# TensorE's order in the token stage of a fused vision-tower kernel: the score in two halves, two turns of z between them, the turned means behind the third turn

## What is computed

```python
# tokenizer: one query per patch, 16 keys and values per patch, 8 heads
reduce_feats = x.mean((3, 5))...                      # mean of each patch
q  = _ln(reduce_feats, ln_q_w, ln_q_b) @ Wq.T
kv = _ln(unf, ln_kv_w, ln_kv_b) @ Wkv.T               # every pixel
attn = softmax(einsum('bhpd,bhpnd->bhpn', q * scale, k))
aggre = einsum('bhpn,bhpnd->bhpd', attn, v)
h = reduce_feats + aggre @ proj_w.T + proj_b
# layer 0
h = h + rnn(_layernorm(h))      # tanh recurrence over the batch of 32
h = h + moe(_layernorm(h))      # 8 experts, 2 per token
```

## Time and profile before

| | before |
|---|---|
| median of 3 runs | 1656.12 us |
| profiled execution, its own time | 1680.15 us |
| its span (first to last instruction) | 1678.3 us |
| token stage, 59 full slots | 95 to 1160 us of the span |
| TensorE busy over the span | 1414.3 us, 84% |
| VectorE, ScalarE, GpSimd busy | 65%, 48%, 42% |
| granted TensorE clock, mean | 0.955 |

### The profile page before, as it was taken

How to read it: one execution, slowest core, us unless ns; L and a number is a source line. 1 busy time by engine, 2 the same in 40 slices (tenths; PEclk the granted TensorE clock), 3 DMA queues, 4 the chain that set the end, 5 groups by cost and what they waited for, 6 DMA issues and landing times. The chain is left out here.

```text
span 1678.3 us, 65455 instructions
## 1 busy us (share of the span) xinstructions
PE 1414.3 (84%) x25781; PEld 1083.8 (65%) x25781; DVE 1099.1 (65%) x3070; ACT 806.3 (48%) x2022; POOL 708.2 (42%) x858
## 2 busy tenths in 40 slices
PE   3799999999998989989898989989648888888870
PEld 2577777777777766777676667677536566555550
DVE  3567666766665767866676667777447556776773
ACT  1365565655554655555555556556443333333330
POOL 1233343333333433356655534334147734332536
PEclk9899999999998999999999999999869999999995
DMA  8977787877776876889999786673257646675866
GB/s 285 345 263 279 249 298 259 301 258 272 283 274 241 306 254 237 296 275 316 317 312 324 268 290 257 218 252 133 76 164 229 220 152 182 201 211 172 251 207 178
DMA packets 202089, 415.69 MB, mean 248 GB/s; under 512 B 25952, under 2 KB 126624, under 8 KB 201664
## 3 DMA queue, kind: packets, MB, share of 16 engines
q1 hardware_dynamic: 187504, 372.69, 64.7%
q0 software_dynamic: 14288, 38.82, 7.8%
HBM read 329.52 MB, written 81.89 MB: 245 GB/s over the span
## 5 line engine op out<-in xcount | busy, mean ns | idle before, releaser
L1039 DVE BATCH_NORM_STATS2 st<-xp 128x6 f32<-128x512 f32 x512 | 339.1, 694 | 0.5
L537 POOL TENSOR_TENSOR rs_px<-px_ve,half_neg 128x16 f32<-128x16 f32 x64 | 186.3, 2911 | 296.8 <-DVE px_ve L1044 296.8
L649 ACT ACTIVATE zT<-bank 128x512 f32<-128x512 f32 x256 | 146.2, 598 | 193.0 <-PE bank L872 192.9
L1332 POOL DMA_INDIRECT y<-ys_dram,slot x130 | 125.3, 964 | 188.4 <-DMA ys_dram<-y_s 84.4
L872 PE MATMUL bank<-ident,z_s 128*128 128x128 f32 x1024 | 163.4, 295 | 28.3 <-issue 27.5
L642 ACT ACTIVATE z_s<-bank 128x512 f32<-128x512 f32 x256 | 138.7, 597 | 61.4 <-PE bank L862 61.4
L623 ACT ACTIVATE u<-bank 128x512 f32<-128x512 f32 x256 | 132.2, 603 | 53.6 <-PE bank L812 53.6
L872 PEld LDWEIGHTS bank<-ident,z_s 128*128 128x128 f32 x1024 | 120.8, 149 | 46.9 <-issue 40.2
L832 PE MATMUL bank<-xc,u 128*32 128x64 f32 x8192 | 133.9, 220 | 18.2 <-issue 17.5
L832 PEld LDWEIGHTS bank<-xc,u 128*32 128x32 f32 x8192 | 128.0, 110 | 32.8 <-issue 21.0
L310 POOL DMA_INDIRECT xs_dram<-xrow,slot x130 | 128.4, 988 | 40.3 <-issue 37.5
(11 more groups left out here) (179 smaller groups left out, 3134.6 us busy)
## 6 DMA issues: line engine op xcount, KB each, us to landing
xp<-xpix SPq DMA_DIRECT2D x256, 512.0 KB
xc<-xg SPq DMA_DIRECT2D x256, 512.0 KB
xt<-xs_dram SPq DMA_DIRECT2D x151, 128.0 KB, 3.3
ys_dram<-y_s SPq DMA_DIRECT2D x151, 128.0 KB, 2.6
xs_dram<-zero SPq DMA_DIRECT2D x49, 384.0 KB, 8.2
base_dram<-h SPq DMA_DIRECT2D x65, 128.0 KB, 7.9
rows_dram<-tok SPq DMA_DIRECT2D x65, 128.0 KB, 7.6
hb<-base_dram SPq DMA_DIRECT2D x65, 128.0 KB, 3.0
```

The costliest lines, as they stand in the source:

```text
L537: pool.tensor_tensor(rs_px[:, :], px_ve[:, :], half_neg[:, :], ALU.pow).then_inc(s["px_done"], 1)
L649: act.activation(zT[:, c, :, :].rearrange("p h (a r t) -> p r h a t", r=2, t=TS)[:, r, :, :, :], BIG[f][:, :].rearrange("p (a h t) -> p h ...
L1039: dve.bn_stats(st[:, j, :], xp[u.x][:, 2 * j:2 * j + 2, :].rearrange("p i c -> p c i")).then_inc(s["st_done"], 1)
```

## The change

Both edits change only an order; no instruction is added or taken away, and no wait.

On TensorE `score` is cut in two calls of 64 matmuls. The waits for its inputs stand in the first, the signal `s_ps` in the second. The order was: means, score, z 0, z 1, rn, z 2, fold, z 3, xn. It becomes: means, score half 0, z 0, z 1, score half 1, z 2, rn, z 3, fold, xn. On ScalarE the copy of z 1 moves ahead of the copy of the turned means.

```diff
@@ ScalarE, slot
                 if back:
                     zT_out(act, w, 0)
+                if back:
+                    zT_out(act, w, 1)
                 if front:
                     rn_out(act, u)
                 if back:
-                    zT_out(act, w, 1)
                     zT_out(act, w, 2)
                     zT_out(act, w, 3)
@@ TensorE
-            def score(pe, u):
-
-                wait_xc(pe, u)
-                wait(pe, s["u_done"], u, 4, 4)
-                wait(pe, s["rep_done"], u, 1, 1)
-                for n in range(4):
+            def score(pe, u, half):
+
+                if half == 0:
+                    wait_xc(pe, u)
+                    wait(pe, s["u_done"], u, 4, 4)
+                    wait(pe, s["rep_done"], u, 1, 1)
+                for n in (2 * half, 2 * half + 1):
...
-                last.then_inc(s["s_ps"], 1)
+                if half == 1:
+                    last.then_inc(s["s_ps"], 1)
@@ TensorE, slot
                 if mid:
-                    score(pe, v)
+                    score(pe, v, 0)
                 if back:
                     turn_z(pe, w, 0)
                     turn_z(pe, w, 1)
+                if mid:
+                    score(pe, v, 1)
+                if back:
+                    turn_z(pe, w, 2)
                 if front:
                     turn_rn(pe, u)
                 if back:
-                    turn_z(pe, w, 2)
+                    turn_z(pe, w, 3)
                 if mid:
                     fold_patches(pe, v)
-                if back:
-                    turn_z(pe, w, 3)
                 if end:
                     turn_xn(pe, z)
```

## The result

The changed kernel takes 1656.51 us (median of 20 runs, 1646.33 to 1664.98). The kernel before, in 20 runs, takes 1664.24 us (1653.06 to 1684.54). The ratio is **0.995**, 95% interval 0.9928 to 0.9971: faster by 0.3 to 0.7%, where 0.8% was forecast. Two numbers of the forecast's base have to be put right at once. The median of before was given as 1656.12 from three runs, and 20 runs put it 8 us higher; the profiled execution of before, 1680.15 us, lies near the top of its spread.

A forecast was written before the change was run, and what follows sets the result against it. The prediction took TensorE's queue as the bound. Gains of 5.1 + 8.6 = 13.7 us took the profiled 1680.15 us to 1666.4, and times 0.9857 to about 1642 us, 0.8% less; range 1626 to 1660.

The forecast's parts named there:

- the bare slot: A token-stage slot undisturbed by instruction fetches: TensorE takes 16.62 us before, forecast 16.3 us after.
- One sign: In the profile after, fold's wait for sm was to be there as often as before or more often.
- The term of 0.34 us: Net gain per undisturbed token-stage slot: xn comes 0.49 us earlier, less 0.15 us at project.
- The 0.15 us: ScalarE copies qT behind the exponentials, so project starts 0.15 us later than values allow.
- The 14.9 packets to five slots: Five slots are 3,590 instructions or 14.9 instruction-fetch packets, so the fetch pattern repeats nearly every five slots.
- The changes of shape: Two more switches a slot between score and transposes on TensorE: up to 0.22 us, covered ahead of fold, taken as 0.
- The sum: Gain of 5.1 us from undisturbed slots plus 8.6 us from the clock, 13.7 us together.
- How many slots get it: Only the 15 undisturbed of 59 token-stage slots gain 0.34 us each: 5.1 us, bounds 0 and 20.1 us.
- The clock: Shorter fetch stops on TensorE spare a third of the falls of the clock in ten slots: 8.6 of 25.7 us.
- The rival of the late edges: 22 fetches asked for in score half 1 come 0.88 us later: 19.4 us lost, 5.1 won, 1670 us; chance 0.12.
- the rival that fetches are hardly ever last without the profiler: All 59 slots gain: 20.1 + 8.6 = 28.7 us, 1628 us, or 1611 with every clock fall spared; chance 0.14.
- the fetch note: TensorE's unnamed idle times are instruction fetches, ending 2.1 to 2.4 us after the packet, whatever TensorE had to do.

The follow-up runs named there:

- quarter loads: From unit 3 (xc) and 4 (xp) on, each load moves a quarter of its bytes: 1608.54 us on the kernel before, 1581.25 us on the changed kernel.
- z 3 alone: Kernel before with only z 3 moved ahead of fold, score whole, rn still ahead of z 2: 1666.77 us, ratio 1.0015 to the kernel before.
- the split alone: Kernel before with only the score cut in two halves, z 0 and z 1 between them, the rest in old order: 1662.0 us, ratio 0.9984.
- the late load: xp load issued right behind the xc load, when the score is through: 1616.84 us on the kernel before, 1611.71 us on the changed kernel.
- spread loads: Same bytes, xc load issued in four parts over the slot, xp in two halves: 1716.92 us on the kernel before, 1702.06 us on the changed kernel.

## Why the prediction was right and wrong

**The sign, the mechanism and the bare slot** held. Fold still waited for VectorE's sm at 6.25 us, rn's wait went, and z 3 left the path. One sign failed: fold's wait was to be listed as often as before, and it is listed 16 times in place of 45, since the turns now fill most of it. The term of 0.34 us was mis-sized: it measures 0.44. The 0.15 us that I took off because qT is copied behind the exponentials is not there: the copy starts at 401.73, 0.09 us ahead of the exponentials' end, lands at 402.34, and project starts at 402.39, just where values end. I had added durations where two ScalarE instructions overlap. And sm comes 1.34 us behind rn, not 1.74 (402.07 - 400.73); nothing rests on it. The 14.9 packets to five slots were worked out with the 241 of the whole span; with 253 they are 14.2, and the pattern of five slots still holds.

**The changes of shape** cost more than the 0.22 us bounded: from the score's start to z 2 it is 3.06 us against 2.78 worked out, 0.28 for two more of them. They lie under the idle time ahead of fold, as said. The rule of the Trainium skill that was weighed (TensorE: Matmul & The Clock Gate, Part 3, The mechanism) has a weight load overlap only where the row group differs, and the prediction drew from it that each change of shape exposes a full load; the trace agrees on the size: 0.14 us for one such change, beside 149 ns for a weight load of the turns on the page of before. The quarter loads show that nothing of it reached the end.

**The sum** is where the prediction failed: 5.1 us for z 3 and 8.6 for the clock, 13.7 together, where 7.7 were measured. Both terms were too large.

**How many slots get it.** Fifteen slots were counted, 5.1 us, as if they stayed bare. The run with z 3 alone tests this term: its interval reaches from 2.3 us gained to 7.3 us lost, and leaves 5.1 gained outside. The profile of the change has 6 slots shorter than 16.4 us, its second profile 6 as well; 6 x 0.44 is 2.6 us. Several slots that were bare are not bare now: the one from 145.4 took 16.6 us, and its counterpart takes 17.4. What z 3 gives within the whole change was not measured by itself. That fetches pin most slots is shown by the quarter loads (27.3 us in place of 7.7) and by the pair of queries above.

**The clock** term was too large as well: a third of 25.7 us, 8.6, and the runs give 1.8 on one chip and 4.2 over all. It was scaled to one profile, and that one lost more to the clock than the kernel usually does: the mean clock of 60 runs of before is 0.960, that of the profile 0.955, and 0.005 x 1660 is 8 us. With quarter loads, where the clock does not fall in the stage, the runs have 0.970; so the falls cost a usual run of before an estimated 0.010 x 1660, 17 us, and a third of that is 5.5. The reason given for the term, falls spared, is not borne out by the count: slots with a clock under 0.95 are 10 in the profile of before, and 9 and 11 in the two of the change, which was named as a sign of being wrong. What they cost is less, 15.4 and 20.5 us in place of 25.7 (length times one minus the clock, as in the prediction), but the profile with z 3 alone, whose runs are no faster, also has 15.4. The stops did get shorter (2.62 to 1.87 us in the slot of the earlier trace rows), but the clock fell in that slot all the same.

**The rival of the late edges** (slower, 1670) fell. Of the fetches asked for in the second half of the score 21 can be paired between the two profiles: TensorE comes to the place from which I took them to be asked for (the start of the block before) some 1.0 us later in the slot, and the packet comes 0.07 us earlier on the mean (0.11 later in the second profile of the change). So the packet's time is set by what stands ahead of it, more than by when it is asked for.

**The base.** 1642 us was 0.9857 times the profiled sum, with 1656.12 as the median of before. With 1664.24 the same gain would have given 1651. The range's low end was set by the rival that fetches are hardly ever last without the profiler; the Trainium skill (Runtime: NRT & Kernel Launch, Instruction fetch mechanics) calls a crossing mostly hidden. For this kernel with full loads it is not: taking three quarters of the bytes away gave 60 us.

**What the fetch note missed.** I had the fetches in the argument as a thing that pins the gain, and did not ask which load stands in front of them. The load of xp at the slot's end was most of the matter: moving it is worth 3.1%, six times the change, or 53.7 of the 60 us that the quarter loads give.

## What to carry to other kernels

When TensorE idles and the trace names no engine, look at the instruction queue's packets and at what transfers were issued just before them: here a large load issued ahead of a dense run of small matmuls starved that run of code. Before tuning the order of the steps, time the loads so that the DMA engines are quiet when the code of the dense run is fetched, and look where they really are quiet. And size a term that depends on rare events from many runs, not from one profile.

## What the hardware showed that was not expected

- TensorE goes on 2.3 and 2.4 us after the packet with its next instructions starts, in the places of the earlier trace rows (packets at 366.79 and 256.63). Over 31 stops of the stage of before it is 2.2 to 2.7 us. By the instruction times the packet starts up to 6 us after TensorE began the block before it. From where it is really asked for no row shows.
- The same bytes in the same number of transfers take 1617 to 1717 us by place of issue alone, with TensorE's order of before (1616.84 and 1716.92).
- Of the falls of the clock to the lower level none is left in the stage with quarter loads, before or after (one slot with the split alone), and none with the late load and the order of before; with spread loads the mean of the stage is 0.96.
